# An edge sort laid out in 128 partitions instead of 125, with its records turned by partition and two one-hot tables on ScalarE

## The chip, the core and the metric

The kernel runs on one core of a Trainium2 chip, in one launch. Its engines are TensorE (PE in the profile, PEld for its weight loads), VectorE (DVE), ScalarE (ACT), GpSimd (POOL) and SyncE (SP). SP, ACT and POOL issue DMAs, which 16 DMA engines carry out. The metric is the device time of one execution in microseconds.

## What is computed

The reference is four layers of a graph network on 3125 nodes of 256 features with 50000 edges. Each layer adds a graph part and a linear attention to the normalized nodes, and then a mixture of experts. All four graph parts sum over edges by destination:

```python
N, D, E = 3125, 256, 50000
src  = randint((E,), 0, N)
dst  = (N * uniform((E,)) ** 2).astype(int32)      # then edges are sorted by dst
...
m     = segment_max(e, dst, num_segments=n)         # layer 0, twice; 2 and 3 alike
ex    = exp(e - m[dst])
denom = segment_sum(ex, dst, num_segments=n)
out   = segment_sum(h[src] * (ex / denom[dst])[:, :, None], dst, num_segments=n)
...
out   = relu(x @ W1.T + segment_sum((x @ W2.T)[src], dst, n))   # layer 1
...
a = leaky_relu(sum((h[src] + edge_attr @ We.T + be) * attn, axis=-1))   # layer 2
```

The kernel therefore first brings the edges into tiles of 128 edges that share one block of 125 destinations. This is the sort that the change touches; it also works out each edge's attribute score `ee` for layer 2.

## The kernel before

The program is a chain of phases with a barrier between each two (line 92 in waits is such a barrier). `sort_edges` (L137 to L607) comes first, right after constants and the load of the nodes; everything behind it reads its result. Nodes are split by P = 125 into NT = 25 blocks, so a destination has a high digit (its block, `hic`) and a low digit (0 to 124, `loc`). The 50000 edges lie in 125 partitions by ER = 400 columns, edge e in partition e // 400. They are treated in NGU = 50 groups of G = 8 columns. The parts:

- **digits** (L185 to L266): loads source, destination and type, makes the digits, turns `dstc` and `loc` by PE and stores them as `dstrows` and `lorows` in memory (one row of 125 for each column), fills the table of records `recs` (TE x 128 = 53248 records of four words) with empty ones (L216), and builds the record columns `rec`.
- **count** (L269 to L331): DVE makes one-hot tables in bf16 for a group (L312, L314), PE multiplies them to a histogram, from which each bin's first position `start` comes.
- **place** (L334 to L474): gives each edge its position and writes its record there. This is a ring of four engines, one step for each group:
  - SP (`load`, L360) loads two rows of a group, broadcast to all partitions (`drow`, `lrow`, L178), as soon as the `eq` instructions have let go of the buffer (`rows_used`), and then the attributes (`ea`, L182) when `attr_used` allows it. Each has two buffers.
  - DVE does for group g the one-hot tables `ohl` (L395), `ohh` (L397) and `oht` (L399); for g-1 the attribute score (L427, L430); for g-2 the position (L438 to L449): it picks the looked-up start, adds the rank and writes `pos` and `stage`. Then come, interleaved eight times, `eq` of group g (L405, equal destinations in lower partitions) and the running sum `run` of g-1 (L422), and last the rank (L434).
  - PE does `count` (L373, `ohl` by `ohh` to `p_delta`) of g and `look` (L379, `oht` by `run` to `p_look`) of g-1, eight matmuls each.
  - POOL (L470) issues eight indirect DMAs a group, each of which scatters 125 records of 16 bytes to `recs`. `pos` and `stage` have four slots; DVE waits for the semaphore `scat` of group g-4 before it writes them (L446). Behind the last group DVE makes a table of tiles by block (L455, L458).
  - ACT has nothing to do here.
- **cols** (L477 to L607): reads `recs` back as `rc`, one record of each tile in each partition (L504), and derives what the edge passes need.

The order of the work on each engine is that of `piped` (L44), which runs each stage with its lag, four steps to a turn of the loop.

## Time and profile before

| | us |
|---|---|
| median of 3 runs | 7957.1 (7951.61 to 7958.37) |
| profiled execution, first to last instruction (span) | 7949.6 |
| digits, until the first load of count | 0 to 50.30 |
| count | 50.30 to 150.24 |
| place, until cols issues its read | 150.24 to 819.11 |
| cols, until its last copy | 819.11 to 883.3 |

The profile is of one execution; the page gives its span and no time of its own beyond that, so the span stands beside the median of the runs. Over the whole span PE is busy for 65%, DVE 63%, ACT 30% and POOL 46%; in `place` alone these shares are others, and the tables by stretch show them. In a timeline each line is one instruction: start, length, engine, line of the code, operation, tiles; in brackets the idle time of the engine just before it and what ended it, where "issue" is time in which the engine waited for nothing that the profile shows. The DMA share in a stretch is that of 16 engines, so that one busy engine is 0.06. TensorE's granted clock is 1.00 in all of the sort, the higher of its two levels.

### The profile page before, as it was taken

The page shows a single profiled execution, that of the slowest core. Times are in us where ns is not written, and L with a number is a line of the kernel's source. Part 1 is how long each engine was busy: PE and PEld are TensorE (multiplying, and loading weights), DVE is VectorE, ACT ScalarE, POOL GpSimd, SP SyncE. Part 2 cuts the span into 40 slices and gives each one's busy share as a digit, 9 for nine tenths or more (in the row PEclk, how much of TensorE's full clock was granted, in tenths as well). Part 3 has the DMA queues.
Part 4 walks back from the last instruction along what each step waited for, and adds up shares of the span by engine and source line. Part 5 has one row for each costly group of instructions (what it writes and reads, how often), then busy time and mean ns, then how long its engine had stood idle before and what let it go on. Part 6 is the DMA issues. An engine that isn't in the chain of part 4 may idle for free. (4 is left out here: it accounts for less than half of the span.)

```text
span 7949.6 us, 108271 instructions
## 1 busy us (share of the span) xinstructions
PE 5184.5 (65%) x21657; PEld 3647.6 (46%) x21658; DVE 4994.5 (63%) x12038; ACT 2383.1 (30%) x5922; POOL 3662.9 (46%) x3784
## 2 busy tenths in 40 slices
PE   4554277747765676675946665776777777776764
PEld 3554144434443654454923344663444444444443
DVE  6787477767776346644166565237999639996453
ACT  0000155325521220001213212223777227772321
POOL 1888277437730146772137720133666116662014
PEclk9999977777787898786956677899999899998787
DMA  1332444324430662334823421774667236772026
GB/s 68 125 126 94 66 125 128 79 67 126 125 61 19 220 214 82 88 90 125 303 62 107 107 45 31 245 229 159 208 209 211 59 108 212 211 211 81 23 92 201
DMA packets 567529, 1020.86 MB, mean 128 GB/s; under 512 B 188186, under 2 KB 328414, under 8 KB 558568
## 3 DMA queue, kind: packets, MB, share of 16 engines
q0 software_dynamic: 191616, 489.64, 22.9%
q1 hardware_dynamic: 345129, 495.90, 19.3%
q10 hardware_dynamic: 30528, 32.52, 1.2%
q8 instruction: 85, 1.39, 0.1%
q14 instruction: 171, 1.40, 0.1%
HBM read 926.84 MB, written 90.26 MB: 128 GB/s over the span
## 5 line engine op out<-in xcount | busy, mean ns | idle before, releaser
L677 POOL DMA_INDIRECT l_hgt_ep_g<-l_tkm,l_hgt_ep_ix x832 | 922.6, 1109 | 445.5 <-PE l_hgt_ep_out L762 241.7
L677 POOL DMA_INDIRECT l_gat_ep_g<-l_gat_th,l_gat_ep_ix x832 | 835.6, 1004 | 240.1 <-issue 230.3
L762 PE MATMUL l_gat_ep_out<-l_gat_ep_g,l_gat_ep_here 128*126 128x264 f32 x1664 | 702.4, 566 | 151.9 <-DVE l_gat_acc L911 142.9
L470 POOL DMA_INDIRECT recs<-place_stage,place_pos x400 | 520.5, 1301 | 143.6 <-issue 135.9
L762 PEld LDWEIGHTS l_gat_ep_out<-l_gat_ep_g,l_gat_ep_here 128*126 128x126 f32 x1664 | 386.9, 263 | 376.7 <-DVE l_gat_acc L911 300.2
L2261 DVE TENSOR_TENSOR f_moe_experts_yb<-f_moe_experts_py,f_moe_experts_b2s 128x256 f32<-128x256 f32 x208 | 88.4, 425 | 718.4 <-PE f_moe_experts_py L2244 703.0
L2212 POOL DMA_INDIRECT f_moe_experts_xg<-f_moe_tx,f_moe_tok x208 | 196.5, 945 | 738.5 <-PE f_moe_experts_px L2225 622.0
L762 PE MATMUL l_hgt_ep_out<-l_hgt_ep_g,l_hgt_ep_here 128*126 128x288 f32 x1664 | 500.5, 424 | 53.0 <-DVE l_hgt_ep_g L897 51.7
L2432 POOL DMA_INDIRECT l_edges_g<-l_table,l_edges_ix x416 | 417.4, 1003 | 180.2 <-issue 100.7
L2235 PE MATMUL f_moe_experts_phid<-f_moe_experts_xt,f_moe_experts_w1b 128*128 128x128 f32 x3392 | 430.7, 282 | 73.4 <-DMA f_moe_experts_b1b<-in_L_ffn_b 62.9
L801 ACT COPY l_gat_ep_stage<-l_gat_ep_out 30x264 f32<-30x264 f32 x832 | 308.0, 371 | 555.8 <-PE l_gat_ep_out L762 543.2
L2276 ACT ACTIVATE f_moe_experts_ht<-f_moe_experts_phid,f_moe_experts_b1b 128x128 f32<-128x128 f32 x848 | 241.3, 372 | 734.9 <-PE f_moe_experts_phid L2235 731.7
L736 PE MATMUL l_hgt_ep_found<-l_q,l_hgt_ep_hot 125*128 x1664 | 427.9, 402 | 38.7 <-ACT l_hgt_ep_hot L777 33.6
L677 POOL DMA_INDIRECT l_ep_g<-l_table,l_ep_ix x416 | 397.0, 954 | 120.0 <-issue 111.7
L2235 PEld LDWEIGHTS f_moe_experts_phid<-f_moe_experts_xt,f_moe_experts_w1b 128*128 128x128 f32 x3392 | 403.6, 195 | 96.5 <-issue 60.1
L2445 PE MATMUL l_edges_out<-l_edges_g,l_edges_here 128*125 128x256 f32 x832 | 271.9, 484 | 205.7 <-DMA l_edges_g<-l_table,l_edges_ix 99.0
L762 PE MATMUL l_ep_out<-l_ep_g,l_ep_here 128*126 128x257 f32 x832 | 333.9, 554 | 108.9 <-DVE l_acc L911 102.3
L2244 PE MATMUL f_moe_experts_py<-f_moe_experts_w2b,f_moe_experts_ht 128*128 128x256 f32 x1696 | 401.6, 381 | 0.0
L911 DVE TENSOR_TENSOR l_gat_acc<-l_gat_acc,l_gat_ep_out 125x264 f32 x832 | 343.8, 413 | 66.2 <-issue 50.2
L911 DVE TENSOR_TENSOR l_hgt_acc<-l_hgt_acc,l_hgt_ep_stage 125x288 f32 x832 | 370.1, 445 | 21.7 <-ACT l_hgt_ep_stage L801 15.4
L801 ACT COPY l_hgt_ep_stage<-l_hgt_ep_out 126x288 f32<-126x288 f32 x832 | 307.8, 394 | 225.8 <-PE l_hgt_ep_out L762 214.1
L762 PEld LDWEIGHTS l_hgt_ep_out<-l_hgt_ep_g,l_hgt_ep_here 128*126 128x126 f32 x1664 | 285.0, 190 | 180.2 <-issue 132.3
(592 smaller groups left out, 11696.2 us busy)
## 6 DMA issues: line engine op xcount, KB each, us to landing
l_hgt_ep_hot<-locrow SPq DMA_DIRECT2D x208, 256.0 KB, 4.8
f_moe_experts_w1b<-in_L_ffn_w SPq DMA_DIRECT2D x32, 1024.0 KB
f_moe_experts_w2b<-in_L_ffn_w SPq DMA_DIRECT2D x32, 1024.0 KB
f_moe_experts_w1b<-in_L_ffn_w SPq DMA_DIRECT2D x64, 512.0 KB
f_moe_experts_w2b<-in_L_ffn_w SPq DMA_DIRECT2D x64, 512.0 KB
f_moe_experts_w1b<-in_L_ffn_W SPq DMA_DIRECT2D x56, 512.0 KB
f_moe_experts_w2b<-in_L_ffn_W SPq DMA_DIRECT2D x56, 512.0 KB
l_gat_ep_hot<-locrow SPq DMA_DIRECT2D x104, 256.0 KB
```

Source lines behind the costliest of these rows:

```text
L470: gp.indirect_dma_start(recs, bass.IndirectOffsetOnAxis(ap=pos[:, b, j:j + 1].bitcast(U32), axis=0), stage[:, b, j, :], None).then_inc(sca ...
L677: gp.indirect_dma_start(g[:, b % NB, j, 0:W], None, table, bass.IndirectOffsetOnAxis(ap=ix[:, b, j:j + 1].bitcast(U32), axis=0)).then_inc( ...
L736: mm = pe.matmul(found[:, h, j * D:j * D + D], hot[0:P, b % 2, 128 * (h * HT + j):128 * (h * HT + j) + 128], look[:, bass.ds(blks[h * HT + ...
L762: pe.matmul(out[:, t % 4, 0:WO], here[:, b % 2, t, :], g[:, b, t, F:F + WO], start=True, stop=True).then_inc(s_out, 1)
L801: act.copy(stage[lo:P + 1, b % 2, t, :], out[lo:P + 1, t % 4, 0:WO]).then_inc(s_staged, 1)
L911: v.tensor_tensor(slot, slot, stage[0:P, b % 2, t, :] if kind == "hgt" else out[0:P, t % 4, 0:WO], ALU.add).then_inc(s_added, 1)
L2212: gp.indirect_dma_start(xg[:, b, :], None, tx, bass.IndirectOffsetOnAxis(ap=tok[:, t:t + 1].bitcast(U32), axis=0)).then_inc(s_x[b], 16)
L2235: mm = pe.matmul(phid[:, b % 2, 128 * f:128 * f + 128], w1b[:, b, k, 128 * f:128 * f + 128], xt[:, b % 2, k, :], start=(k == 0), stop=(k = ...
L2244: mm = pe.matmul(py[:, b % 2, 0:D], ht[:, b % 2, f, :], w2b[:, b, f, :], start=(f == 0), stop=(f == FC - 1))
L2276: act.activation(ht[:, b % 2, f, :], phid[:, b % 2, 128 * f:128 * f + 128], func, bias=b1b[:, b, f:f + 1])
L2432: gp.indirect_dma_start(g[:, b, j, :], None, table, bass.IndirectOffsetOnAxis(ap=ix[:, b, j:j + 1].bitcast(U32), axis=0)).then_inc(s_g[b], 16)
L2445: pe.matmul(out[:, j, 0:D], here[:, i % 4, j, :], g[:, i % RB, j, :], start=True, stop=True).then_inc(s_out, 1)
```

## The change

Edges lie in 128 partitions. 390 columns (WHOLE) are full; the 80 edges left go into column 390, and the columns are filled up to EC = 392, which are NGU = 49 groups of 8. Places without an edge get destination N = 3125, which has the high digit 25: so there is one bin more, NH = 26. Their record's destination is set to -1, as for the empty records. Every load of the place part, every table and each scatter have 128 partitions (`run` and `p_delta`, which are by digit, stay at 125).

`recs` is laid out by partition: 128 rows of TE + 1 = 417 records. The position s of an edge becomes (s mod 128) x 417 + s // 128, for which `place` gets three more small instructions on DVE. The read of `rc` then is contiguous in each partition.

The tables `ohl` and `oht` are made on ScalarE, as Relu(1 - |x|): eight Abs with a bias for each column and one Relu, and one Abs and one Relu. PE waits for these by two more semaphores, SP waits for `turned_hot` before it loads rows again, and DVE waits for the rows only at its first `eq`.

```diff
+NH = NT + 1
+WHOLE = E // 128
+EC = -(-E // 1024) * 8
...
-    recs = core.dram("recs", (TE * 128, 4), I32)
+    recs = core.dram("recs", (128 * (TE + 1), 4), I32)
...
-    NGU = ER // G
+    NGU = EC // G
...
-        drow = keep2.sb("drow", [P, 2, G * P])
-        lrow = keep2.sb("lrow", [P, 2, G * P])
-        ea = keep2.sb("ea", [P, 2, G, 128])
+        drow = keep2.sb("drow", [128, 2, G * 128])
+        lrow = keep2.sb("lrow", [128, 2, G * 128])
+        ea = keep2.sb("ea", [128, 2, G, 128])
...
-                sp.dma_start(sbt[:, b, :], rows[bass.ds(g * G, G), :].rearrange("t p -> (t p)").partition_broadcast(P)
+                sp.dma_start(sbt[:, b, :], rows[bass.ds(g * G, G), :].rearrange("t p -> (t p)").partition_broadcast(128)
...
+                    sp.wait_ge(blank, 3)
+                    for dst, src in ((si, "src"), (di, "dst"), (ti, "edge_type_2")):
+                        sp.dma_start(dst[0:LEFT, WHOLE:WHOLE + 1], ins[src][128 * WHOLE:E].rearrange("(p o) -> p o", o=1)).then_inc(loaded, 16)
...
-                sp.dma_start(recs.rearrange("(p t) w -> p t w", p=128), pad[:, :, :]).then_inc(stored, 16)
+                sp.dma_start(recs.rearrange("(p t) w -> p t w", p=128)[:, 0:TE, :], pad[:, :, :]).then_inc(stored, 16)
...
                         sp.wait_ge(rows_used, g + 1)
+                        sp.nop(nofuse=True)
+                        sp.wait_ge(turned_hot, g - 1)
+                        sp.nop(nofuse=True)
                         load_rows(sp, g, b)
...
                     pe.wait_ge(hot, g + 1)
+                    pe.wait_ge(low_hot, g + 1)
...
                     pe.wait_ge(runs, G * (g + 1))
+                    pe.wait_ge(turned_hot, g + 1)
...
+            @block.scalar
+            def _(act):
+                def digit_hots(g, b):
+                    if later(g, 4):
+                        act.wait_ge(delta, g - 3)
+                    for j in range(G):
+                        act.activation(ohl[:, b, j, :], core.iota[:, 0:P], ACT.Abs, bias=minusloc[:, bass.ds(g * G + j, 1)])
+                    act.drain()
+                    act.activation(ohl[:, b, :, :], ohl[:, b, :, :], ACT.Relu, bias=core.ones[:, 0:1], scale=-1.0).then_inc(low_hot, 1)
+
+                def turned_hots(g, b):
+                    act.wait_ge(rows_in[b % 2], 32 * (g // 2 + 1) if isinstance(g, int) else 16 * (g - b % 2 + 2))
+                    if later(g, 4):
+                        act.wait_ge(looked, g - 3)
+                    act.activation(oht[:, b, :, :].rearrange("p g e -> p (g e)"), lrow[:, b % 2, :], ACT.Abs, bias=core.minusp[:, 0:1])
+                    act.drain()
+                    act.activation(oht[:, b, :, :], oht[:, b, :, :], ACT.Relu, bias=core.ones[:, 0:1], scale=-1.0).then_inc(turned_hot, 1)
+                piped(act, NGU, [(0, digit_hots), (0, turned_hots)])
...
-                    v.wait_ge(rows_in[b % 2], 32 * (g // 2 + 1) if isinstance(g, int) else 16 * (g - b % 2 + 2))
                     if later(g, 4):
-                        v.wait_ge(looked, g - 3)
-                    v.tensor_tensor(ohl[:, b, :, :], core.iota[0:P, 0:P].unsqueeze(1).to_broadcast([P, G, P]),
-                                    loc[:, bass.ds(g * G, G)].unsqueeze(2).to_broadcast([P, G, P]), ALU.is_equal)
...
-                    v.tensor_scalar(oht[:, b, :, :].rearrange("p g e -> p (g e)"), lrow[:, b % 2, :], core.iotap[0:P, :], None, ALU.is_equal
-                                    ).then_inc(hot, 1)
+                        v.wait_ge(delta, g - 3)
...
+                        if j == 0:
+                            v.wait_ge(rows_in[b % 2], 32 * (g // 2 + 1) if isinstance(g, int) else 16 * (g - b % 2 + 2))
...
                     v.tensor_tensor(posf2[:, :], posf[:, :], rank[:, b, :], ALU.add)
                     v.drain()
+                    v.tensor_scalar(posf[:, :], posf2[:, :], -63.5, 1.0 / 128, ALU.add, ALU.mult)
+                    v.drain()
+                    v.tensor_scalar(tile[:, :], posf[:, :], ROUND, -ROUND, ALU.add, ALU.add)
+                    v.drain()
+                    v.scalar_tensor_tensor(out=posf[:, :], in0=tile[:, :], scalar=-128.0, in1=posf2[:, :], op0=ALU.mult, op1=ALU.add)
+                    v.drain()
...
-                    v.tensor_copy(pos[:, b, :], posf2[:, :])
+                    v.scalar_tensor_tensor(out=pos[:, b, :], in0=posf[:, :], scalar=float(TE + 1), in1=tile[:, :], op0=ALU.mult, op1=ALU.add)
...
-            sp.dma_start(rc[:, :, :], recs.rearrange("(t p) w -> p t w", p=128)).then_inc(loaded, 16)
+            sp.dma_start(rc[:, :, :], recs.rearrange("(p t) w -> p t w", p=128)[:, 0:TE, :]).then_inc(loaded, 16)
```

On DVE, one step of `place` ran from the tables of a group to the writing of an older group's positions in this order before (`place_ohl`, `place_ohh`, `place_oht` are the one-hot tables, `place_prod` the attribute products, `place_lk` and `place_posf` the looked-up position):

```order
L395 TENSOR_TENSOR place_ohl<-keep_iota,prep_lo 125x1000 [waits prep_rows_in0]
L397 TENSOR_TENSOR place_ohh<-keep_iota,prep_hi 125x200
L399 TENSOR_SCALAR place_oht<-prep_lrow,keep_iotap 125x1000
L427 TENSOR_TENSOR place_prod<-prep_ea,prep_wea 125x1024 [waits prep_attr_in1]
L430 TENSOR_REDUCE place_ee<-place_prod 125x8
L438 TENSOR_TENSOR place_lk<-place_look,place_ohh 125x200 [waits place_looked]
L440 TENSOR_REDUCE place_posf<-place_lk 125x8
L442 TENSOR_TENSOR place_posf<-place_posf,place_rank 125x8
L447 CAST place_pos<-place_posf 125x8
L448 COPY place_stage<-prep_rec 125x8x3
L449 TENSOR_SCALAR place_stage<-place_ee,prep_wea 125x8
```

The same stretch of DVE now:

```order
L445 TENSOR_TENSOR place_ohh<-keep_iota,prep_hi 128x208
L475 TENSOR_TENSOR place_prod<-prep_ea,prep_wea 128x1024 [waits prep_attr_in1]
L478 TENSOR_REDUCE place_ee<-place_prod 128x8
L486 TENSOR_TENSOR place_lk<-place_look,place_ohh 128x208 [waits place_looked]
L488 TENSOR_REDUCE place_posf<-place_lk 128x8
L490 TENSOR_TENSOR place_posf<-place_posf,place_rank 128x8
L492 TENSOR_SCALAR place_posf<-place_posf 128x8
L494 TENSOR_SCALAR place_tile<-place_posf 128x8
L496 SCALAR_TENSOR_TENSOR place_posf<-place_tile,place_posf 128x8
L501 SCALAR_TENSOR_TENSOR place_pos<-place_posf,place_tile 128x8
L502 COPY place_stage<-prep_rec 128x8x3
L503 TENSOR_SCALAR place_stage<-place_ee,prep_wea 128x8
```

Two tables and the wait for the rows have left the step's head, and three small instructions stand ahead of the write of `place_pos`.

On ACT, which had no instruction in `place` before, this now stands for each group (here the first two):

```order
L422 ACTIVATE place_ohl<-keep_iota,prep_minuslo 128x125 x8
L424 ACTIVATE place_ohl<-place_ohl,keep_ones 128x1000
L430 ACTIVATE place_oht<-prep_lrow,keep_minusp 128x1024 [waits prep_rows_in0]
L432 ACTIVATE place_oht<-place_oht,keep_ones 128x1024
L422 ACTIVATE place_ohl<-keep_iota,prep_minuslo 128x125 x8
L424 ACTIVATE place_ohl<-place_ohl,keep_ones 128x1000
L430 ACTIVATE place_oht<-prep_lrow,keep_minusp 128x1024 [waits prep_rows_in1]
L432 ACTIVATE place_oht<-place_oht,keep_ones 128x1024
```

The low-digit table of a group stands behind the turned table of the group before, which waits for its rows.

## Rows read from the trace of the kernel before

**Rows 1.** The one core: span, mean granted TensorE clock.

```profile
core 0: 7949.6 us, clock 0.847
```

**Rows 2.** Timeline ahead of `place`, and its start.

```profile
44.44 0.60 SPq L216 DMA_DIRECT2D recs<-digits_pad  x1
50.30 0.28 SPq L178 DMA_DIRECT2D prep_drow<-dstrows  x1
...
150.24 0.29 DVE L388 COPY place_run<-prep_start 125x25 f32<-125x25 f32 x1 [0.50 <-PEq L92]
...
172.46 1.47 POOL L470 DMA_INDIRECT recs<-place_stage,place_pos  x1 [21.97 <-issue]
```

**Rows 3.** Timeline at the end of `place` and behind it.

```profile
765.22 10.98 DVE L455 TENSOR_TENSOR place_ct<-place_io,prep_tstart 1x10400 f32<-1x10400 f32 x1
765.43 11.83 POOL L470 DMA_INDIRECT recs<-place_stage,place_pos  x1 [0.30 <-issue]
...
813.37 1.18 POOL L470 DMA_INDIRECT recs<-place_stage,place_pos  x1 [0.30 <-issue]
819.11 0.40 SPq L504 DMA_DIRECT2D cols_rc<-recs  x1
...
851.90 0.53 DVE L549 CAST cols_dcol<-cols_rc 128x416 f32<-128x416 int32 x1 [31.77 <-DMA cols_rc<-recs]
```

**Rows 4.** POOL's indirect DMAs by line: ns min/median/max, first and last start.

```profile
L470 POOL DMA_INDIRECT recs<-place_stage,place_pos x400: 1182/1187/11832, 172.5 to 813.4; - x134
...
L677 POOL DMA_INDIRECT l_gat_ep_g<-l_gat_th,l_gat_ep_ix x832: 942/946/2012, 946.4 to 2276.1; - x167
...
L1755 POOL DMA_INDIRECT f_out_y<-f_moe_ty,f_moe_pos x175: 1191/1207/1460, 2895.2 to 7940.4; - x175
```

**Rows 5.** Timeline of one step of `place`, DVE and POOL.

```profile
401.57 1.20 DVE L395 TENSOR_TENSOR place_ohl<-keep_iota,prep_lo 125x1000 f32<-125x1000 f32 x1 [1.35 <-DMA prep_lrow<-lorows]
...
402.69 0.36 DVE L397 TENSOR_TENSOR place_ohh<-keep_iota,prep_hi 125x200 f32<-125x200 f32 x1
402.97 0.74 DVE L399 TENSOR_SCALAR place_oht<-prep_lrow,keep_iotap 125x1000 f32<-125x1000 f32 x1
403.62 1.22 DVE L427 TENSOR_TENSOR place_prod<-prep_ea,prep_wea 125x1024 f32<-125x1024 f32 x1
...
404.35 1.54 POOL L470 DMA_INDIRECT recs<-place_stage,place_pos  x1 [0.30 <-issue]
...
406.93 0.17 DVE L442 TENSOR_TENSOR place_posf<-place_posf,place_rank 125x8 f32<-125x8 f32 x1
407.17 0.19 DVE L447 CAST place_pos<-place_posf 125x8 int32<-125x8 f32 x1
...
408.95 0.34 DVE L405 SCALAR_TENSOR_TENSOR place_eq<-prep_drow,prep_dst,keep_low 125x125 f32<-125x125 f32 x1
409.19 1.19 POOL L470 DMA_INDIRECT recs<-place_stage,place_pos  x1 [0.30 <-issue]
...
413.74 1.20 DVE L395 TENSOR_TENSOR place_ohl<-keep_iota,prep_lo 125x1000 f32<-125x1000 f32 x1 [1.67 <-DMA prep_lrow<-lorows]
```

**Rows 6.** Waits in `place`: engine, line, waited for, us in total, times, longest.

```profile
DVE place_ohl L395 <- DMA prep_lrow<-lorows: 78.1, 46, 3.0
```

**Rows 7.** Stretches: busy us of PE, PEld, DVE, ACT, POOL; clock, DMA share, GB/s.

```profile
400.00:400.50 0.50, 0.50 (x5) 0.50 (x4) 0.22 (x1) 0.00 (x0) 0.20 (x1) 1.00 0.32 115
...
360.00:460.00 100.00, 57.26 (x258) 55.31 (x258) 81.80 (x247) 0.00 (x0) 80.80 (x64) 1.00 0.38 126
...
3780.00:3800.00 20.00, 20.00 (x137) 18.62 (x136) 1.68 (x5) 6.51 (x24) 2.54 (x3) 1.00 0.97 342
```

**Rows 8.** ACT's instructions by line: busy us, mean ns, idle before.

```profile
L783 ACT ACTIVATE l_hgt_ep_here<-keep_iota,keep_e_minusrow 128x126 f32<-128x126 f32 x832 | 261.1, 385 | 0.0
...
L777 ACT ACTIVATE l_gat_ep_hot<-l_gat_ep_hot,keep_ones 128x1024 bf16<-128x1024 bf16 x104 | 119.4, 1148 | 7.2
```

**Rows 9.** The page's DMA issues: KB each, us to landing.

```profile
l_hgt_ep_hot<-locrow SPq DMA_DIRECT2D x208, 256.0 KB, 4.8
```

157 lines of the change are left out of this document (89 added, 68 removed).

## The prediction

> **What bounds the kernel now.** I read the spans first: one core, 7949.6 us from first to last instruction [rows 1]. Then I looked for the stretch that the change touches. The sort runs from 0 to 883 us, with barriers between its parts, and all that follows waits for its result, so what the sort saves the kernel saves. Its costliest part is `place`, from 150.24 us [rows 2] to the last scatter at 813.37 + 1.18 us [rows 3]. There the groups of instructions and the waits show two chains that run nearly equally fast.
>
> POOL issues 400 scatters of 125 records, and its idle time is 0.30 us before nearly each, which is no wait: median 1.187 us [rows 4] + 0.30 [rows 3] = 1.49 us, 11.9 us for the eight of a group. From 172.46 [rows 2] to 814.55 it takes 642.1 us, of which 400 x 1.187 + 399 x 0.302 = 595.3; the other 46.8 are stretched scatters.
>
> DVE takes 12.17 us a step: its table instruction L395 starts at 401.57 and again at 413.74, after 1.67 us idle that ended with the load of `prep_lrow` [rows 5]; 46 such waits total 78.1 us [rows 6]. So the loads pace DVE. Each group loads two tiles of 125 x 1000 words and one of 125 x 1024, 1.51 MB, which in 12.2 us is 124 GB/s, and the stretches show 126 GB/s throughout, with a DMA share of 0.32 in a moment between scatters [rows 7]. Five of sixteen engines are 0.31: loads of 125 partitions seem to use five engines, all the time. The weight loads, on 128 partitions, reach 342 GB/s at a share of 0.97 [rows 7]. DVE finishes its last group just before 765.22 us, POOL 50 us later [rows 3], so **POOL sets the end of the part**, and DVE would be next at nearly the same price. PE waits for DVE.
>
> **POOL after the change.** Group count: 392 columns of 128 make 49 groups, 392 scatters instead of 400. Price of one: the trace has no scatter of 128 rows. Gathers of 128 rows take 0.946 us and gathers of 125 rows 1.207 us, and the 125-row scatter lies with the latter, at 1.187 [rows 4]. The number of rows decides, not the direction; I take 0.945, bounds 0.945 and 1.187. With the 0.302 us between: 392 x 1.247 = 488.8 us.
>
> The stretched scatters have a pattern. The scatter at 404.35 started while DVE's two-tile instruction L427 ran (403.62 to 404.84) and took 1.54, ending 1.05 after it [rows 5]; L455, 10.98 us long at 765.22, held the scatter at 765.43 for 11.83 [rows 3]. The scatter at 409.19 started during L405 (408.95 to 409.29) and took 1.19 [rows 5]. So TENSOR_TENSOR on two SBUF tiles blocks a scatter that starts during it (L395 and L427 are the long ones), the others do not. L395 leaves DVE; L427 stays. A start falls into L427's 1.22 us about once a group; the block lasts between 0 and 1.09 us, 0.5 taken: 24.5 us over 49 groups (bounds 0 and 53). L455 stays: 10.9 us. POOL's chain: 488.8 + 24.5 + 10.9 = 524.2 us, against 642.1: **117.9 us less**.
>
> The Trainium skill (SBUF — State Buffer, "SBUF: two separate sides") says that DVE and GpSimd share a port pair, and that an operation in a two-port mode or with two SBUF inputs holds it for the whole instruction. By that, L405, which reads two tiles for eight times 0.34 us a group, would hold up scatters too, some 0.4 us a group or 19 us more. The scatter at 409.19 does not show it, and I stay with the row [rows 5].
>
> **DVE after the change.** From 12.17 us: the wait goes (1.67), if the loads are faster. L395 and L399 go to ACT: start to start 1.12 and 0.65 us [rows 5]. `place` gets three more dependent small instructions; from L442 to L447 is 0.24 us [rows 5], so + 0.72. Wider tiles (128 for 125, 208 for 200 columns) add some 0.1. Together 12.17 - 1.67 - 1.77 + 0.82 = **9.55 us a step**, less than POOL's 524.2 / 49 = 10.7 (10.5 without L455). So DVE runs ahead until the wait on the slots of scatter holds it, and POOL stays fed. The new cover is thin: beyond 10.5 us a step, DVE would set the end.
>
> **ACT and PE.** ACT is empty in this part. It gets eight Abs of 128x125, one Relu of 1000 and two of 1024 a group. The nearest rows are 0.385 us for 128x126 from the same `iota`, and 1.148 us for 128x1024 [rows 8]: 3.1 + 3.4 + drains 0.4 = 6.9 us, hidden under DVE's step. PE now waits for three producers. Its `count` of a group stands behind `look` of the group before, and `run_on` needs it only one step later; ACT makes the tables for the next group while it waits for nothing but rows that were issued two steps earlier. No cost, bounds 0 and 2 us a step, which are in the second rival.
>
> **Loads after.** 1.57 MB a group in 10.5 us asks for 150 GB/s. With sixteen engines 342 GB/s have been seen, 4.6 us. The loads have only to stay below 10 us: they need not reach that rate, but they must beat today's 126 GB/s.
>
> The Trainium skill (DMA: Bandwidth & Descriptors, "Why a DMA increments its semaphore by 16 and not by 1") gives the number of engines as the largest up to 16 that divides the slowest dimension: 5 for 125, 16 for 128. The share of 0.31 agrees for 125. By the rule the step is DVE's 9.55; if instead the broadcast stayed at five engines' rate, the third rival's time would come.
>
> **Before and behind `place`.** The digits phase gets three more small DMAs before DVE can start. An issue by SP takes 0.60 us at 44.44 [rows 2], and each may take longer behind a full queue: + 3 us (bounds 1 and 5). `count` has 49 turns instead of 50 (barrier to barrier 50.30 to 150.24 [rows 2], so up to 2.0 us each), each about 0.01 longer: - 1.4. In `place`, DVE's way to the first scatter is 22.2 us (150.24 to 172.46). Three times 1.77 us and a wait of 0.7 go, 0.72 comes: 17.2. ACT's first tables (6.9 us a group) are ready at step 1, just in time. First scatter at about 150.24 + 1.6 + 17.2 = 169.0 instead of 172.46: **3.5 us earlier** (bounds 0 and 6).
>
> Behind it, `cols_rc` is read back. SP issues at 819.11 and DVE gets it at 851.90 [rows 3], 32.8 us for 852 KB in pieces of 16 bytes, 26 GB/s. Turned by partition it is 128 pieces of 6656 bytes. The store of the same 832 KB in that form, issued at 44.44, was over by 50.30, barrier included [rows 2]: 5.8 us at most. **27 us less** (bounds 26 and 29). All else behind the sort has the same instructions and the same order of records.
>
> **Sum.** 117.9 + 3.5 + 27 = 148.4 us from 7949.6 makes 7801.2; the median of the runs is 7.5 us above that span, so **7808.7 us**, 1.87% less.
>
> **Rivals.** *DVE, ACT or PE sets the pace.* The new waits (`low_hot`, `turned_hot`) or longer ACT instructions make a step of 11.5 us. The last scatter then ends at 169.0 + 48 x 11.5 + 10 + 10.9 = 742 instead of 814.6: 72.6 + 27 = 99.6 less, 7857 us. For it: cover of 0.9 us only, four engines in one ring. Against: ACT's 6.9 us. Chance 0.12.
> *A scatter of 128 records costs as one of 125.* 392 x 1.489 + 24.5 + 10.6 = 618.8, 23.3 less; with 3.5 and 27 it is 53.8 less, 7903 us. Only the direction speaks for it. Chance 0.06.
> *The loads stay at 124 GB/s.* 1.573 MB then take 12.7 us a group: 169.0 + 48 x 12.7 + 21 = 800, 15 less; with 27, 7915 us. Chance 0.05.
> *Slower than before.* The lrow/drow broadcasts, 128 readers of one 4 KB row on all engines at once, crawl. The nearest row is `l_hgt_ep_hot`, a broadcast of 256 KB that lands after 4.8 us beside gathers [rows 9], 55 GB/s as it stands, though most of that may be latency. It decides from the point where 169.0 + 48 x P + 21 exceeds 814.6 + 27: P = 13.6 us, 116 GB/s. At 15 us a step it would be 7957 + 68 = 8025 us. Chance 0.03.
> The forecast keeps 0.74.
>
> **How the numbers follow.** The forecast's own range: stretches 0 to 53 us in place of 24.5 (- 24.5, + 28.5), the scatter held by L455 avoided (- 10.9), ends - 2 and + 5: 7772 to 7842. To hold 0.8 it has to reach the first rival, with steps up to nearly 12 us: 7772 to 7875. A measurement of this kernel tells about 0.2%, 16 us, from no change. Faster by more than that: the forecast and three rivals hold 0.97, of which I leave 0.02 to the same for what I don't see (a changed clock of TensorE behind the sort): faster 0.95, same 0.02, slower 0.03.
>
> **What would show it.** The scatters: a median of 0.94 to 0.95 us with 0.30 between (wrong at 1.19). The wait of DVE for `prep_lrow` gone from the list, GB/s in the part at about 150. A step of 10.2 to 10.8 us, POOL without real idle time, DVE waiting at the write of `place_pos`. ACT busy 6 to 7.5 us a step. The read of `cols_rc` in under 6 us. If POOL idles for `placed`, the first rival holds, and the engine that DVE waits for names it. If the part ends later than 720 us, the forecast is wrong.

## The result, and the profile after

| | kernel before | changed kernel |
|---|---|---|
| time, median of 4 runs each, same chip | 7954.35 us (7950.32 to 7958.37) | 7816.6 us (7811.16 to 7820.44) |
| ratio after / before | | 0.9819, 95% interval 0.9806 to 0.9833 |
| span of the profiled execution | 7949.6 us | 7816.4 us |
| start of `place` | 150.24 us | 146.77 us |
| first scatter | 172.46 us | 165.94 us |
| last scatter ends | 814.55 us | 710.11 us |
| SP issues the read of the records | 819.11 us | 720.21 us |
| DVE has them | 851.90 us | 725.65 us |

The forecast was 7808.7 us; the time lies 8 us above it, well inside the range. The spans differ by 133.2 us: 126.2 of it has been won when DVE has the records, against 148.4 forecast for the whole; the rest of the sort gives 1.5 back, and all behind the sort is 8.4 us shorter without having been touched. Those 8.4 us are no gain of the change: in four traces at this level of kernels with the change (this one, `e7`, `e8` and `e9` below), all with the same code behind the sort, that part took 7044 to 7062 us, and 7066 in the kernel before.

Granted TensorE clock of the one core, from the list of spans [rows 1 before]:

```profile
core 0: 7816.4 us, clock 0.846
```

The start, from the timeline, to set beside [rows 2]: the load ahead of `count`, the copy that starts `place`, the first scatter.

```profile
48.17 0.37 SPq L185 DMA_DIRECT2D prep_drow<-dstrows  x1
...
146.77 0.18 DVE L439 COPY place_run<-prep_start 125x26 f32<-125x26 f32 x1 [0.84 <-DVEq L94]
...
165.94 1.18 POOL L524 DMA_INDIRECT recs<-place_stage,place_pos  x1 [19.26 <-DVEq L504]
```

The end of `place`, from the timeline, to set beside [rows 3]: the long table operation of DVE and the scatter it holds, the last scatter, the read, and its arrival.

```profile
661.56 10.98 DVE L509 TENSOR_TENSOR place_ct<-place_io,prep_tstart 1x10400 f32<-1x10400 f32 x1
...
662.72 10.66 POOL L524 DMA_INDIRECT recs<-place_stage,place_pos  x1 [0.30 <-issue]
...
709.15 0.96 POOL L524 DMA_INDIRECT recs<-place_stage,place_pos  x1 [0.30 <-issue]
720.21 0.34 SPq L558 DMA_DIRECT2D cols_rc<-recs  x1
...
725.65 0.53 DVE L603 CAST cols_dcol<-cols_rc 128x416 f32<-128x416 int32 x1 [4.43 <-DMA cols_rc<-recs]
```

All scatters by their line (ns min/median/max, first and last start), to set beside [rows 4]. The median has fallen from 1187 to 958 ns.

```profile
L524 POOL DMA_INDIRECT recs<-place_stage,place_pos x392: 954/958/10658, 165.9 to 709.1; - x196
```

One step of DVE and POOL, from the timeline, to set beside [rows 5]. Start to start of L501 it is 11.12 us, of which DVE waits 1.51 for a slot of `place_pos`. Two of the scatters shown are not 0.96 us long: the one at 403.48 started 0.18 us before the end of an L453 and took 1.02; the one at 406.07 started 0.09 us into L475 and took 1.96.

```profile
400.68 0.17 DVE L501 SCALAR_TENSOR_TENSOR place_pos<-place_posf,place_tile 128x8 int32<-128x8 f32 x1 [1.63 <-DMA recs<-place_stage,place_pos]
...
403.32 0.34 DVE L453 SCALAR_TENSOR_TENSOR place_eq<-prep_drow,prep_dst,keep_low 128x128 f32<-128x128 f32 x1
403.48 1.02 POOL L524 DMA_INDIRECT recs<-place_stage,place_pos  x1 [0.30 <-issue]
...
405.98 1.22 DVE L475 TENSOR_TENSOR place_prod<-prep_ea,prep_wea 128x1024 f32<-128x1024 f32 x1
406.07 1.96 POOL L524 DMA_INDIRECT recs<-place_stage,place_pos  x1 [0.30 <-issue]
...
408.33 0.95 POOL L524 DMA_INDIRECT recs<-place_stage,place_pos  x1 [0.30 <-issue]
...
411.80 0.17 DVE L501 SCALAR_TENSOR_TENSOR place_pos<-place_posf,place_tile 128x8 int32<-128x8 f32 x1 [1.51 <-DMA recs<-place_stage,place_pos]
```

The waits of 160 to 700 us (engine, line, waited for: us in total, times, longest). DVE's wait for `prep_lrow` of [rows 6] is gone; DVE now waits for POOL's slots, and the engine that waits for the rows is ScalarE, which has the time.

```profile
ACT place_oht L430 <- DMA prep_lrow<-lorows: 198.3, 45, 5.8
...
POOL recs L524 <- issue: 114.9, 377, 0.3
DVE place_pos L501 <- DMA recs<-place_stage,place_pos: 39.4, 27, 2.2
```

Two stretches (busy us of PE, PEld, DVE, ACT, POOL; clock, DMA share, GB/s), the second to set beside the second of [rows 7]: 143 GB/s in place of 126, and 170 while DVE runs ahead to fill the slots.

```profile
160.00:260.00 100.00, 74.25 (x343) 72.99 (x343) 88.45 (x306) 64.24 (x123) 73.33 (x69) 1.00 0.53 170
...
360.00:460.00 100.00, 63.02 (x290) 61.89 (x290) 78.92 (x275) 53.58 (x104) 77.76 (x73) 1.00 0.44 143
```

ScalarE's instructions in `place` by line (busy us, mean ns, idle before), to set beside [rows 8]. Eight of L422 run in 2.41 us; with the three others a group takes some 5.9 us, where 6.9 was forecast.

```profile
L422 ACT ACTIVATE place_ohl<-keep_iota,prep_minuslo 128x125 f32<-128x125 f32 x369 | 111.2, 384 | 0.0
L432 ACT ACTIVATE place_oht<-place_oht,keep_ones 128x1024 f32<-128x1024 f32 x47 | 53.9, 1148 | 3.2
L430 ACT ACTIVATE place_oht<-prep_lrow,keep_minusp 128x1024 f32<-128x1024 f32 x47 | 53.9, 1147 | 198.3 <-DMA prep_lrow<-lorows 198.3
L424 ACT ACTIVATE place_ohl<-place_ohl,keep_ones 128x1000 f32<-128x1000 f32 x47 | 53.0, 1128 | 3.8 <-issue 0.4
```

### The profile page after: what moved, and what is told of

It is laid out like the page before. It is cut to its first block and busy times, and to the rows that moved or that the text cites. A ratio compares the mean times of both kernels' runs of the same rounds, so it can differ in the third digit from the quotient of the medians.

```text
span 7816.4 us, 109527 instructions
## 1 busy us (share of the span) xinstructions
PE 5146.3 (66%) x21617; PEld 3624.5 (46%) x21618; DVE 4929.8 (63%) x12062; ACT 2667.4 (34%) x6461; POOL 3569.9 (46%) x3776
## 5 line engine op out<-in xcount | busy, mean ns | idle before, releaser
L816 PE MATMUL l_gat_ep_out<-l_gat_ep_g,l_gat_ep_here 128*126 128x264 f32 x1664 | 686.0, 554 | 160.9 <-DVE l_gat_acc L965 152.4
L524 POOL DMA_INDIRECT recs<-place_stage,place_pos x392 | 425.0, 1084 | 138.5 <-issue 117.4
L790 PE MATMUL l_hgt_ep_found<-l_q,l_hgt_ep_hot 125*128 x1664 | 426.4, 400 | 38.3 <-ACT l_hgt_ep_hot L831 33.3
```

Of the source, the lines that this page charges most:

```text
L524: gp.indirect_dma_start(recs, bass.IndirectOffsetOnAxis(ap=pos[:, b, j:j + 1].bitcast(U32), axis=0), stage[:, b, j, :], None).then_inc(sca ...
L790: mm = pe.matmul(found[:, h, j * D:j * D + D], hot[0:P, b % 2, 128 * (h * HT + j):128 * (h * HT + j) + 128], look[:, bass.ds(blks[h * HT + ...
L816: pe.matmul(out[:, t % 4, 0:WO], here[:, b % 2, t, :], g[:, b, t, F:F + WO], start=True, stop=True).then_inc(s_out, 1)
```

## Where POOL's 544 us go

POOL's chain, first start to last end, is 544.2 us: 392 x 0.958 + 391 x 0.305 = 494.8, and 49.4 in scatters that are longer than the median. I went through all 392 in the timeline and noted which of DVE's instructions ran at the start of each:

| DVE's instruction at the scatter's start | its inputs | scatters | us over the median, in sum |
|---|---|---|---|
| L475, product for the score, 1.22 us | two tiles in SBUF | 47 | 32.2 |
| L509, last table, 10.98 us | two tiles in SBUF | 1 | 9.7 |
| L453, comparison of nodes, 0.34 us | two tiles in SBUF | 64 | 7.3 |

Nearly all the longer ones start in one of these three. The three rows make 49.2 of the 49.4 us; the rest is the first scatter, 0.2 us longer. L475 starts before L445 has ended, and a scatter that starts while both run is put to L475, since it loses some 1.0 us, more than the 0.36 of L445. L445, the table of the high digit, reads two SBUF tiles too, but held none here; in `e4_psum_all` below it held 20, for 3.3 us. The reductions (L478, L482) held none of the 94 scatters that started in them; operations on one tile and those that read PSUM (L470, L486) held none for their own length. The extra time is what is left of DVE's instruction, less some 0.13 us. In L453 95 scatters started; of the 31 that weren't held 21 had less than 0.14 us of it left, and ten began in its first 0.05 us.

## The experiments

Twelve kernels ran, on three chips: `e1` to `e4` on the first, `r1`, `r2`, `e5` and `e6` on the second, `e7` to `e10` on the third. The first two ran the whole program some 560 us slower, the kernel before too (8520.08 and 8509.75 us there, 7952.56 on the third); the third was at the level of the result above. So only totals of one chip are compared, and otherwise the times inside `place`, which in the kernel before were the same within 2 us on both kinds of chip. TensorE's granted clock was 1.00 in the sort on both kinds, and lower over the whole run on the slower ones (0.815 in `r2_before_again`, 0.847 in the first trace).

### The number of records in a scatter

`e1_scatter125`, the changed kernel with one difference; the records of the last three partitions are left out:

```
-  IndirectOffsetOnAxis(ap=pos[:, b, j:j + 1]...), stage[:, b, j, :]
+  IndirectOffsetOnAxis(ap=pos[0:125, b, j:j + 1]...), stage[0:125, b, j, :]
```

> The changed kernel, but each scatter names 125 of the 128 partitions, so the records of three partitions are left out. Theory (what counts is whether the records of one scatter divide over the 16 DMA engines): median scatter back at 1.19 us from 0.958, so POOL's chain in place grows by 392 x 0.23 = 90 us to about 634 us, kernel near 7905 us. Rival (the cheaper scatter comes from the new layout of recs or from the wider loads beside it, not from the count): median stays at 0.95 to 0.96, kernel near 7815.

Measured: 8472.33 us, beside 8520.08. Its scatters, by line:

```profile
L524 POOL DMA_INDIRECT recs<-place_stage,place_pos x392: 1182/1187/10632, 166.2 to 772.3; - x196
```

The old price to the nanosecond, with everything else changed. POOL's chain is 607.2 us, and POOL never waits. The expectation had 634: the median came as expected, but the longer scatters add 22.8 us in place of 49.4. So the shorter scatter comes from the count of records alone. Behind the last one, SP's read is issued 3.8 us later; in the changed kernel it is 10.1 us (710.11 to 720.21), and 4.6 us before.

`e10_scatter112` does the same with 112 partitions, in a kernel whose loops in `place` are written out (below). The records of 16 partitions are left out, so its other stages and its total of 7907.83 us say nothing.

> The kernel with all loops of the place written out, but each scatter sends the records of 112 partitions (a multiple of 16), not 128: the records of 16 partitions are left out. The scatter of 125 records took 1.187 us and that of 128 takes 0.958. Theory: what counts is that the records divide into 16 equal shares; then 112 takes 0.93 to 0.96 us. Rival: only the full 128 partitions are cheap, or the price is one step up for anything less; then 112 takes 1.1 to 1.2 us. The drain of POOL's queue behind the last scatter tells too: 3.8 us for 125 records, 10.1 for 128.

```profile
L531 POOL DMA_INDIRECT recs<-place_stage,place_pos x392: 937/942/10652, 166.1 to 696.7; - x196
```

942 ns: an eighth fewer records than 128 save 16 ns, while 125 cost 229 ns more than 128. It is not the full width that counts but that the records divide well: the rival of a price for anything below 128 falls, and the theory of equal shares stands. Which divisor is enough isn't shown, for 112 is also a multiple of 2, 4 and 8, and no multiple of these that isn't one of 16 was run. The Trainium skill (DMA: Bandwidth & Descriptors, "Why a DMA increments its semaphore by 16 and not by 1") says that a transfer uses the largest number of engines up to 16 that divides its slowest dimension, 5 for 125 and 16 for 112 and 128; the order of the three prices agrees with it. How many engines a scatter used, no row shows.

### The loads

`e2_narrow_loads`: the three loads of a group as one of 125 partitions and one of 3, and waits to fit.

```
+  for lo, hi in ((0, 125), (125, 128)):
-    sp.dma_start(sbt[:, b, :], rows[...].partition_broadcast(128))
+    sp.dma_start(sbt[lo:hi, b, :], rows[...].partition_broadcast(hi - lo))
```

> The changed kernel, but each load of rows and attributes is split into one of 125 partitions and one of 3, so that the bytes, tables and scatters are the same. Theory (125 partitions use five DMA engines, and that paced DVE before): traffic falls back to about 125 GB/s, a step takes 12.6 us, POOL idles for DVE, and place ends about 48 x 12.6 us after its first scatter: near 800 instead of 720 us, kernel near 7890 us. Rival (the loads only wait in line because DVE asked for them late; any shape would do): step stays at 10.9 us, kernel near 7817.

Measured: 8460.81 us, chain 636.8 us. One stretch of it:

```profile
360.00:460.00 100.00, 55.78 (x256) 54.78 (x256) 69.47 (x240) 44.75 (x87) 68.85 (x64) 1.00 0.33 125
```

Share 0.33 and 125 GB/s, evenly over the whole stretch, as in the kernel before: one partition set of 125 puts the load back on a third of the engines. In the changed kernel the loads come in bursts, in which single microseconds show 381 to 427 GB/s, with pauses. So this term of the prediction stands. The length of the chain, 12.6 us a group expected and 13.0 measured, isn't to be laid to the loads alone: on this chip another delay is in it (below), and the total even came out below those of the next two.

### The operations that hold a scatter

`e3_psum_wea`: the score's second operand, 128 weights a partition, is copied to PSUM once ahead of the loop and read from there.

```
+  p_wea = ph.psum("wea", [128, 128])
+  v.tensor_copy(p_wea[:, :], wea[:, 0:128])
-  v.tensor_tensor(prod, ea[:, b % 2, :, :], wea[:, 0:128]...
+  v.tensor_tensor(prod, ea[:, b % 2, :, :], p_wea[:, :]...
```

> The changed kernel, with the weight row wea that DVE's attribute product reads held in PSUM instead of SBUF, so that this instruction has one SBUF input. Theory (an instruction of DVE with two SBUF inputs holds up a scatter that starts during it): the 44 scatters of 1.6 to 2.0 us vanish, 29 us less on POOL's chain (544 to 515), kernel near 7788. Rival (it is DVE's long instructions as such, or the load that SP issues just then): the stretched scatters stay, kernel near 7817.

`e4_psum_all`: the same, and the second operand of L453 and of L509 too.

> As e3, and also the lower-triangle mask of the eight eq instructions and the start row of the last table in PSUM, so that no long instruction of DVE beside the scatters has two SBUF inputs but the one-hot table of 0.37 us. Theory: besides the 29 us, the 64 scatters longer by 0.12 us (7.5 us) and the one held for 10.7 us go, in all 46 us less than the changed kernel on POOL's chain (544 to 498 us), kernel near 7771. If DVE reads PSUM more slowly and its step grows above 10.1 us, part of it is lost: up to 49 x 0.5 us. Rival (eq does not hold up scatters): 39 us less, the 1.02 to 1.12 us scatters stay.

Measured: 8501.12 us and 8497.43 us (ratio to before 0.9979, 0.9965 to 0.9994). The holds went as foreseen. The scatters of `e4_psum_all`:

```profile
L530 POOL DMA_INDIRECT recs<-place_stage,place_pos x392: 952/958/1183, 165.9 to 808.2; - x196
```

The longest is 1.18 us, where it was 10.66. Summed, the scatters take 378.8 us, that is 3.3 over 392 medians; in `e3_psum_wea` 391.1, of which the one during the last table has 10.2. DVE's product still takes 1.21 us: the operation isn't shorter, it only no longer keeps POOL waiting. That reading two tiles of SBUF is the cause is shown.

But the totals didn't fall, and the chains were 655.6 and 643.2 us where 515 and 498 had been expected, since POOL had gaps of some 6 us after every sixteenth scatter, 145 us in sum in both. That was the surprise, and the next runs are about it.

### The changed kernel again, on such a chip

> The changed kernel itself, on the chip of the other runs of this call. In the first experiments (records of 125 partitions scattered, loads narrowed, score weights in PSUM, all second operands in PSUM) the whole kernel took 8461 to 8501 us beside 8520 for the kernel before, and in three of the four SP issued the loads of every second group 2.5 to 6.5 us after DVE's release, POOL then waiting some 5 to 6 us in every second group. Two theories. If that lateness comes from the chip or its load, the changed kernel shows it here too: SP's lag behind the last L453 alternates between 0.7 and several us, POOL has gaps of 5 us after every sixteenth scatter, and the ratio to before is about 0.997. If it comes from what those kernels changed, the lag is 0.63 to 0.72 us in every group as in the trace of after, POOL's chain of scatters takes 544 us within 5, and before minus after is 138 us within 15 whatever the level of the rest.

> The kernel before, unchanged, for its trace beside the others of this call. Its place stage should repeat the first trace: scatters of 1.187 us, first scatter near 172.5, POOL's chain 642 us, the read of the records 32.8 us. What the total lies above 7954 us is then in the stages behind the sort, which all kernels of this call share.

| | before, first trace | r2_before_again | after, first trace | r1_after_again |
|---|---|---|---|---|
| time | 7954.35 | 8506.84 | 7816.6 | 8463.33 |
| POOL's chain | 642.1 | 643.9 | 544.2 | 622.4 |
| of it between scatters | 121.6 | 121.6 | 119.2 | 190.0 |
| read of the records issued | 819.11 | 822.43 | 720.21 | 798.32 |
| span behind that | 7130 | 7683 | 7096 | 7651 |

The ratio there is 0.9946 (0.9927 to 0.9965): 46 us in place of 138, and the 78 us that POOL's chain is longer account for most of the difference. The theory that the delay came from the edits of `e1` to `e4` falls; the changed kernel has it on such a chip as it stands. Two waits of `r1_after_again` from 170 to 700 us:

```profile
DVE place_lk L486 <- remote: 111.6, 21, 7.7
...
POOL recs L524 <- DVEq L504: 64.1, 19, 5.5
```

and the pattern, from the timeline, SP and the last L453 of a group, by which DVE releases the rows:

```profile
560.31 0.34 DVE L453 SCALAR_TENSOR_TENSOR place_eq<-prep_drow,prep_dst,keep_low 128x128 f32<-128x128 f32 x1
...
561.05 0.21 SPq L185 DMA_DIRECT2D prep_drow<-dstrows  x1
...
563.50 0.33 SPq L193 DMA_DIRECT2D prep_ea<-in_edge_attr  x1
...
569.95 0.34 DVE L453 SCALAR_TENSOR_TENSOR place_eq<-prep_drow,prep_dst,keep_low 128x128 f32<-128x128 f32 x1
...
573.17 0.02 SPq L185 DMA_DIRECT2D prep_drow<-dstrows  x1
```

At 561.05 SP follows 0.40 us after the release at 560.65; at 573.17 it is 2.88 us late. In the first trace of the changed kernel the lag is 0.36 us or less in every group but the first two (0.63 to 0.72 in the expectation, which counts to the end of the issue).

What is late at 573.17 is neither of the two things that SP waits for. DVE let go at 570.29, and ScalarE's table had been ready since 568.70. SP's own records show the rest: it was past both waits at 570.47, and then its next two instructions, a register operation and a move, took 0.71 and 0.73 us. By line, for the loads of rows (ns min/median/max; the kernel on the chip of the result first, then `r1_after_again` and `e3_psum_wea`):

```profile
L185 SPq MOVE prep_lrow<-lorows x43: 29/29/29, 178.1 to 614.2; - x43
L185 SPq MOVE prep_lrow<-lorows x43: 6/440/729, 179.0 to 711.5; - x43
L185 SPq MOVE prep_lrow<-lorows x43: 14/697/737, 182.5 to 744.3; - x43
```

Between the first scatter and the last, 94 of SP's 422 instructions took 0.6 to 0.8 us in `r1_after_again`, 133 to 143 in `e2` to `e5`, 28 in `e6_tables_on_dve` and 5 in `e1_scatter125`, where POOL never waits; in the first traces of both kernels and in `r2_before_again` there is none. So SP is slow in single instructions there, each by some 0.7 us.

It isn't the place in the loop. In `r1_after_again` the late groups are nearly all the even ones, which stand first behind the branch at the end of SP's loop of two groups; in `e3_psum_wea` and `e4_psum_all` they are the odd ones, second in the pass, and in `e5_no_turn` first the odd and later the even.

Then everybody is late in turn: in the other half of the pass DVE's L486 waits 5 to 8 us for something that the profile can't name ("remote"), and POOL runs out of places. The kernel before, with 12.2 us a step and no third wait in SP's loop, has a lag of 0.17 or 0.18 us in every group on the same chip, and its moves take 29 ns each: it doesn't hide the slow instructions, it has none in `place`. Why not, these runs don't show.

### Parts of the change, on the same chip

`e5_no_turn`: the records stand in the order of tiles again, DVE's three operations for the turned place are gone, and the read gathers.

```
-  sp.dma_start(rc[:, :, :], recs.rearrange("(p t) w -> p t w", p=128)[:, 0:TE, :])
+  sp.dma_start(rc[:, :, :], recs[0:128 * TE, :].rearrange("(t p) w -> p t w", p=128))
```

> 128 partitions and the ScalarE tables, but the records stand in memory in the order of tiles, as before, and the read gathers them; DVE's three operations for the turned place are gone. By the theory of the prediction the turn is worth the read alone: the read of the records takes 32 to 33 us again in place of 5.4 (+27), the scatters stay at 0.958 us and the chain at 544 us within 5. The drain of POOL's queue behind the last scatter, 2.7 us before and 8.5 after, tells two theories apart: if it is the price of writing 128 records at 128 far addresses it falls back to about 2.7 here, if it belongs to scatters of 128 records it stays near 8.5.

Measured: 8510.33 us. The read is issued at 806.63 us and DVE has the records at 839.97: 33.3 us in place of 5.6 in `r1_after_again`. So the turn is worth 27.7 us at the read. The scatter's median is 959 ns: where the records go costs nothing there. The last scatter ends at 796.5, the read follows 10.1 us later: the longer drain belongs to the scatter of 128 records, not to the scattered addresses. (The 2.7 and 8.5 us of the expectation are POOL's drain instruction alone; the stretch from the last scatter to the read is 4.6 and 10.1.) The chain is 631.4 us; with the delay of that chip in it (POOL idles 94 us beyond its issue), I read nothing from the 9 us against `r1_after_again`.

`e6_tables_on_dve`: both tables are made by DVE again, and ScalarE, with SP's third wait, is out.

```
-  act.activation(ohl[:, b, j, :], core.iota[:, 0:P], ACT.Abs, bias=minusloc[...])
+  v.tensor_tensor(ohl[:, b, :, :], core.iota[:, 0:P]..., loc[...]..., ALU.is_equal)
+  v.tensor_scalar(oht[...], lrow[:, b % 2, :], core.iotap[:, :], None, ALU.is_equal)
```

> 128 partitions and turned records, but both one-hot tables are made on DVE again, 1.20 us and 0.74 us for a group as before. Theory: they cost twice. DVE's step of 9.55 us becomes 11.5 us, longer than eight scatters without holds (8 x 1.263 = 10.1), so that DVE sets the pace: 47 x 11.6 = 545 us plus what the holds add, and the new operation on two inputs (1.20 us) holds one scatter in most groups. Chain 570 to 600 us against 544. Rival: the places are made four groups ahead, POOL never waits for DVE, and the chain grows only by the holds of one more operation, 48 x 0.4 = 19 us, to about 563, with POOL waiting for nothing but its own issue.

Measured: 8427.57 us in one run, 36 below the median of the changed kernel on the same chip, and 1 below its fastest of ten. The read is issued at 781.18 us, 17 earlier, though the scatters sum to 453.0 us, that is 77 of holds against 57. The chain is 602.3 us; SP's lag is 0.17 us in all groups but one, and POOL's idle time beyond its issue falls from 71 to 30 us. The expectation, 570 to 600 us for DVE as the pace, was missed by 2 us and not met in its rule: were DVE the pace, POOL would wait in every group, but its gaps come in every third or fourth. The rival's 563 us is missed by 39. As far as one trace of each tells, the tables on ScalarE don't pay in `place` on this chip: the chain is 20 us shorter without them. Of SP's instructions 28 took 0.6 to 0.8 us, where there were 94 in `r1_after_again`, though its loop branches back as before. Whether that comes of the third wait that is gone from the loop, of ScalarE out of the ring or of DVE's longer step isn't separated. On the chip of the result that pair wasn't run, so what the ScalarE tables are worth there stays open.

### Loops written out, and a version that is faster

`e7_sp_straight`: SP's loop in `place` written out.

```
-  each(sp, NGU, load, peel=True)
+  for g in range(NGU): load(g, g % 2)
```

> The changed kernel with one difference: SP's loop over the 49 groups of the place (two groups in each pass) is written out, so SP never branches back there; the other engines keep their loops of four groups. In the repeat of the changed kernel SP issued the loads of every second group 3.1 us after DVE's release in place of 0.7, always in the half of its loop that stands behind the branch back, and POOL's chain took 622 us in place of 544. Theory: what SP needs to go on behind its branch, about 10 us there, is the cause, and it is now the pace of two groups (25.3 us) because the stage has become faster. Then the lag is 0.6 to 0.8 us in every group here, POOL's gap of 3 to 5 us after every sixteenth scatter goes, and the chain is 545 to 585 us (PE's and DVE's own branches every fourth group remain). Rival: the DMA queues or the memory are slower there; then straight code changes nothing, and the chain stays within 5 us of 622.

`e8_all_straight`: the loops of PE, ScalarE, DVE and POOL in `place` too.

> As the last, and the place loops of PE, ScalarE, DVE and POOL are written out too. Theory of the branches: chain 540 to 550 us as in the first trace of the changed kernel (392 x 0.958 + 391 x 0.305 = 495, holds 40 to 50), POOL waits for nothing but its issue, ScalarE waits for the rows alone. Rival: straight code has its own price, in that each engine must fetch new instructions all the time; then DVE and SP show waits of a microsecond or more spread over all groups and the chain lies above 570.

Measured: 7817.74 us and 7805.96 us beside 7952.56, one run each. These two ran on a chip at the level of the result, where the delay doesn't exist, so they don't tell its theories apart. What they show is that straight code has no price in `place`: SP's lag is 0.12 us in nearly every group, and the chains are 541.6 and 536.0 us (540 to 550 expected for the second). The 8 us against 544.2 are holds: the product of the score holds 47 scatters in each, for 29.8 and 22.4 us in place of 32.2, since they start at another moment of it. POOL waits for nothing beside its issue.

`e9_psum_straight`: all loops written out, and the three operands in PSUM.

> All loops of the place written out, and DVE's three operations that read two tiles in SBUF while scatters start (the score's product, the comparison of nodes, the last table) take one of them from PSUM. With the branches gone and the holds gone nothing is left beside the scatters: 392 x 0.958 + 391 x 0.305 = 495 us for the chain, plus 3 to 10 for the little holds of L445; POOL waits for its issue alone. If ScalarE (6.9 us), PE (7.1 us) or DVE's step of 9.55 us and its waits for freed slots set the pace instead, the chain stays at 49 x 10.8 = 530 or more. Against the kernel before, on a chip where the changed kernel's ratio is 0.995: 117 + 45 = 160 to 175 us less, ratio 0.980 to 0.982; where it is 0.982: ratio 0.975.

Measured: **7763.23 us** (7754.55 to 7782.06), ratio to before 0.9768 (0.9746 to 0.979; 0.975 expected): the fastest of all. Its scatters, and one of them beside the product of the score:

```profile
L537 POOL DMA_INDIRECT recs<-place_stage,place_pos x392: 954/958/1183, 166.0 to 661.5; - x196
```

```profile
407.62 1.21 DVE L488 TENSOR_TENSOR place_prod<-prep_ea,place_wea 128x1024 f32<-128x1024 f32 x1
408.36 0.96 POOL L537 DMA_INDIRECT recs<-place_stage,place_pos  x1 [0.30 <-issue]
```

The scatter at 408.36 starts in the middle of the product and takes its 0.96 us. The chain is 496.5 us: 392 medians and 391 pauses and 1.7 us. That is the floor of this chain but for 1.7 us, where I had allowed 3 to 10. Against `e8_all_straight`, which differs by the three operands alone, it is 39.5 us less. DVE is busy 91 of 100 us there; its own step is 9.5 us where POOL's is 10.1, so it is the next bound, and not far off.

## Why the prediction was right, and where it wasn't

| step of the prediction | forecast | measured |
|---|---|---|
| POOL's scatters and pauses | 488.8 | 494.8 |
| scatters held, without the last table | 24.5 | 39.7 |
| scatter held by the last table | 10.9 | 9.7 |
| first scatter earlier | 3.5 | 6.5 |
| read of the records | -27 | -27.35 |
| last scatter to the issue of the read | no change | +5.5 |
| rest of the sort | no change | +1.5 |
| behind the sort | no change | -8.4 |
| span | -148.4 | -133.2 |

**The mechanism was right**: POOL set the end of the part, its scatters became cheaper, and the loads ceased to pace DVE. In the first twenty groups, while DVE waits for no slot, its step is 9.4 to 9.9 us, where 9.55 had been forecast; from then on the slots hold it to POOL's 11 us. The loads moved 143 GB/s; the read took 5.4 us where 5.8 had been the bound.

**The closeness of the total is in part luck.** In the span the forecast was 15 us too far down (148.4 against 133.2), and without the 8.4 us behind the sort, which are no effect of the change, it would be 24. The time came within 8 us because the forecast added 7.5 us, the distance from span to median in the kernel before, and in the changed kernel that distance was 0.2. Three of the prediction's own signs came out just beside it: the median of a scatter is 0.958 us (0.94 to 0.95), the step 11.1 us (10.2 to 10.8), ScalarE's work 5.9 us (6 to 7.5). The part ended at 710.11 us by the last scatter, as the prediction counts it, under its mark of 720; the read behind it was issued at 720.21, because of the drain below.

**The scatter, 0.958 us in place of 0.945.** I took the price of a gather of 128 rows for that of the scatter. 392 times 13 ns and 3 ns a pause make the 6 us. That the count of records decides is shown by `e1_scatter125`, and that it needn't be the full 128 by `e10_scatter112`.

**The held scatters, 39.7 us in place of 24.5.** Two errors in one term. The first is the mean of 0.5 us a group for the product: starts of scatters aren't spread evenly over it. 47 scatters, nearly one a group, start inside L475, mostly 0.44 us into it and otherwise near 0.09 or 0.80, and lose 0.68 us each on average. That nearly every group has one follows from the lengths, 1.22 us for the product and 1.26 from start to start of the scatters; why they gather at three places isn't shown. DVE waits for slots that scatters free, but in the kernel before, where it waited for loads, 47 starts lay together as well, at 0.73 to 0.86 us. The second is the step where I let [rows 5] speak against the Trainium skill (SBUF — State Buffer, "SBUF: two separate sides") on L405. The scatter at 409.19 started 0.24 us into an operation of 0.34 us. With 0.10 us left it couldn't show a hold, as the holds are shorter than the time left by some 0.13 us. The row told nothing, and I read it as a no. The same trace had the answer: of 55 scatters that start inside L405, 23 are longer, by 1.8 us in sum. After the change 64 scatters start inside L453 with more left, and lose 7.3 us. The estimate by the Trainium skill's rule in the prediction was 19 us, 0.4 us a group; the rule, that an operation of DVE on two SBUF inputs holds the port for its whole length, agrees with the held scatters of the table by DVE's instructions, and with `e4_psum_all` and `e9_psum_straight`, where one input in PSUM ends it.

**The first scatter, 6.5 us in place of 3.5.** The three additional loads in `digits` were set at 3 us. SP issues them from 29.27 to 31.56 us, 2.3 us, but DVE started 1.2 us earlier than before (36.01 against 37.19). The trace puts the end of its wait down to a load of `digits_ti`, one of which is among the three; what made up for them is that SP's issues ahead of them were shorter in this trace (0.43 us for the destinations in place of 0.97). `digits` came out 2.1 us shorter, `count` 1.3 (forecast 1.4), DVE's way to the first scatter 3.1. The forecast of that way, 17.2 us, has a slip: 22.2 - 5.31 - 0.7 + 0.72 is 16.9, and 19.2 were measured.

**The drain.** I had set what lies between POOL's last scatter and the read at nothing. It grew from 4.6 to 10.1 us, and POOL's own drain instruction behind its last scatter from 2.7 to 8.5. The runs put it to the count of records: 3.8 us with 125, 10.1 with 128 whether turned or not (`e5_no_turn`, `e6_tables_on_dve`, `e9_psum_straight`), 8.1 with 112. In `e4_psum_all` it is 12.3, with the same 8.5 us in POOL, since there DVE's last table is what ends last. That the cheaper scatters leave more behind them that has still to land fits this, but what is queued wasn't measured.

**The rivals.** None came true on the chip of the result. On the slower chips the first rival did in part: POOL waited for places, the step was 12.7 us (622.4 / 49), and the gain was 46 us, where the rival had forecast 100. But the engine that these traces show late was none of the three that it names; it was SP, with single instructions of 0.7 us. My sum had a cover of 0.9 us a step for waits in the new ring, and the point against the rival was ScalarE's 6.9 us alone. SP wasn't in the argument, though it got a third wait.

**Still open** is why single instructions of SP take 0.7 us there. The fetching of code comes to mind. The Trainium skill (Runtime: NRT & Kernel Launch, "Instruction fetch mechanics") says that a branch taken out of the two blocks an engine holds makes it stop to fetch. No run here shows it: the kernels with the loops written out ran on a chip without the delay. Against the branch as the cause speak the late groups that are second in the pass (`e3_psum_wea`, `e4_psum_all`), and `e6_tables_on_dve`, where SP branches as often and all groups but one follow in 0.18 us or less. It also isn't shown why these chips need 550 us more behind the sort, in the kernel before as well; but the same thing occurs there. From 900 us on about 900 of SP's instructions take 0.6 to 0.8 us in the kernel before and in the changed one (897 and 890), and so do 141 and 143 of DVE's sequencer, waits and drains left out; in the first traces it is 441 and 440 of SP's, and 3 and none of DVE's.

## What to carry to other kernels

Give a scatter or a load a number of rows that is a multiple of sixteen, as far as these counts tell: 112 records cost 0.942 us and 128 cost 0.958, but 125 cost 1.187, and loads of 125 partitions use a third of the DMA. Beside a POOL that issues indirect DMAs without pause, let DVE read one of its two inputs from PSUM where that costs nothing; it was worth some 40 us on the chip of `e9_psum_straight`, and nothing to be seen in the total where SP was late (`e4_psum_all`). And before a row is taken as proof against a rule, see whether that row could have shown the rule's effect at all.

## What was not expected of the hardware

- The same kernel gained 138 us on one chip and 46 on another, with the kernel before's `place` equal on both within 2 us. On the second single instructions of SP, moves that take 29 ns on the first, took 0.7 us. What sets the pace of a tight ring can change from chip to chip.
- Scatters of 128 records return to POOL 0.23 us earlier than those of 125, but 5.5 us more lie behind the last one.
- Scatters don't start evenly over DVE's product: of 47, most start 0.44 us into it, and the rest near 0.09 or 0.80.
- A one-input operation of DVE held no scatter: in the kernel before nine started in L399 (0.74 us), each with 0.71 us of it left, and none was longer than the median by more than 2 ns.
